# A transformer layer with experts on one core: feed-forward output as three split products, compact denominators, key epsilon by summed values, and a new order of each batch's work

## The reference

```python
xp = einsum(x * norm, proj); diag = sum(x**2) * 0.5 * norm**2      # per head
stab = max(xp, -1) if is_query else max(xp, (-1, -2))
feature = ratio * (exp(xp - diag - stab) + EPS_K)                  # EPS_K = 1e-4; qp, kp
k_sum = sum(kp, tokens); denom = qp . k_sum; ctx = kp^T v
out = (qp . ctx) / denom
x = layer_norm(video + out @ Wo.T + bo, g2, be2)
ff = relu(x @ W1.T + b1) @ W2.T + b2
x = layer_norm(x + ff, g3, be3)
```

## Time and profile before

| | |
|---|---|
| median of 3 runs | 826.82 us (825.84 to 826.87) |
| the profiled execution | 828.11 us, span 826.1 us |
| mean granted clock of TensorE | 0.917 |
| busy, share of the span | PE 85%, DVE 74%, ACT 57%, POOL 45% |
| starts of batches 0, 1, 2, 4 and 7 on TensorE | 14.13, 77.52, 135.76, 253.70, 430.41 us |
| last feed-forward's first hidden chunk | 493.47 us |
| selection | 538.3 to 599 us |
| experts, then the last normalisation | from 599 us |

### The profile page before, as it was taken

One profiled execution on the slowest core, in us unless ns is written; L12 is line 12 of the kernel. 1 busy time (PEld: TensorE's weight loads), 2 busy tenths in 40 slices (PEclk: granted clock), 3 DMA queues, 4 the chain that ended last, 5 costly groups with the idle time before them and its releaser, 6 DMA issues. The chain is left out here.

```text
span 826.1 us, 15455 instructions
## 1 busy us (share of the span) xinstructions
PE 703.9 (85%) x5669; PEld 571.6 (69%) x5669; DVE 612.1 (74%) x1279; ACT 474.6 (57%) x753; POOL 370.1 (45%) x364
## 2 busy tenths in 40 slices
PE   4777999999999999999999979632599999999930
PEld 3655867868768768768768758522488899998830
DVE  4637659878978978978888797777776777678671
ACT  2553674875875875866867834354055444455461
POOL 4065341662564544536527512400244565454673
PEclk9867999999999999999999999755599999999975
DMA  7000001012012011011011011250136644556694
GB/s 244 2 2 26 2 2 52 1 52 70 10 52 78 0 69 59 25 51 52 25 51 28 27 52 52 66 174 0 46 116 154 157 113 112 133 149 160 155 236 100
DMA packets 50700, 60.97 MB, mean 74 GB/s; under 512 B 9312, under 2 KB 44896, under 8 KB 50656
## 3 DMA queue, kind: packets, MB, share of 16 engines
q1 hardware_dynamic: 42400, 46.45, 17.3%
q0 software_dynamic: 7296, 13.77, 8.8%
q10 hardware_dynamic: 960, 0.17, 0.1%
HBM read 39.28 MB, written 21.10 MB: 73 GB/s over the span
## 5 line engine op out<-in xcount | busy, mean ns | idle before, releaser
L1907 PE MATMUL pF<-w,h 128*128 128x256 f32 x448 | 106.0, 382 | 0.0
L1004 POOL DMA_INDIRECT kp<-row_scratch,idx_g x32 | 41.5, 1298 | 117.5 <-issue 60.3
L1907 PEld LDWEIGHTS pF<-w,h 128*128 128x128 f32 x448 | 81.8, 190 | 13.1 <-issue 3.4
L793 ACT ACTIVATE h<-pX,b1cur 128x512 f32<-128x512 f32 x64 | 44.1, 689 | 62.9 <-DVE b1cur L1697 45.6
L2205 PE MATMUL pX<-w_lo,h_hi 128*128 128x256 f32 x256 | 73.2, 286 | 0.8 <-issue 0.8
L2205 PE MATMUL pX<-w_hi,h_lo 128*128 128x256 f32 x256 | 72.4, 283 | 0.0
L2205 PE MATMUL pX<-w_hi,h_hi 128*128 128x256 f32 x256 | 72.4, 283 | 0.0
L881 POOL TENSOR_SCALAR ve<-mv 128x4 f32<-128x4 f32 x36 | 8.5, 235 | 140.6 <-DVE mv L1082 139.5
L1653 DVE TENSOR_TENSOR h_lo<-h,h_hi 128x512 fp32r<-128x512 f32 x64 | 42.9, 690 | 29.3 <-ACT h_hi L785 29.3
L1012 POOL DMA_INDIRECT acc_scratch<-qp,idx_s x28 | 53.1, 1897 | 22.6 <-DVE qp L1679 18.3
L1844 PE MATMUL pX<-x2T_hi,w_lo 128*128 128x512 f32 x128 | 51.6, 403 | 1.6 <-DVE x2T_lo L1723 1.6
(11 more groups left out here) (375 smaller groups left out, 2098.2 us busy)
## 6 DMA issues: line engine op xcount, KB each, us to landing
kp<-fc1T SPq DMA_DIRECT2D x8, 1024.0 KB
w<-fc2T SPq DMA_DIRECT2D x8, 1024.0 KB
xin<-video SPq DMA_DIRECT2D x8, 512.0 KB, 3.8
x<-video SPq DMA_DIRECT2D x7, 512.0 KB, 4.5
out<-x SPq DMA_DIRECT2D x7, 512.0 KB, 3.0
acc_scratch<-xf SPq DMA_DIRECT2D x7, 512.0 KB, 2.9
row_scratch<-y SPq DMA_DIRECT2D x7, 512.0 KB, 3.0
kp<-acc_scratch SPq DMA_DIRECT2D x4, 512.0 KB, 6.5
```

The source lines that it names most:

```text
L793: nc.scalar.activation(h[:, n, :], pM[n % M_SLOTS], ACT.Gelu_apprx_tanh, bias=b1cur[:, n:n + 1]).then_inc(he_ready, 1)
L1004: pool.indirect_dma_start(xg[:, g, :], None, row_d, bass.IndirectOffsetOnAxis(ap=idx_g[:, g:g + 1], axis=0)).then_inc(gathered, 16)
L1907: ins = nc.tensor.matmul(pF[m][:, half * D:(half + 1) * D], h[:, k, tok(2 * m + half)], w2[:, k, :], start=(k == 0), stop=(k == FC - 1))
```

## The change

1. The feed-forward output becomes three split products in the experts' form: `h_hi*w2_lo` and `h_hi*w2_hi` (`ff_top`), later `h_lo*w2_hi` (`ff_low`), 96 fp32r products of 128x256 a batch. ScalarE makes `h_hi` (eight copies of 128x512), VectorE `h_lo` over `h` (eight subtractions, `rest_of_hidden`, in the order `low(n)`); `w2` is split once in batch 0. The end stage does the same in half width.
2. Denominators of all heads go into one 128x128 tile (nine groups of four products), one reciprocal follows, and a selector product spreads it over `pX`; ScalarE copies the outputs out of PSUM, VectorE multiplies.
3. The key epsilon is no longer added to `kp`: GpSimd sums the four value slices (`vsum`, 128x512 and 128x256), and the contexts and the denominators get a group of products with an epsilon column.
4. Each engine's order is new, below for VectorE, GpSimd and TensorE. SP loads inputs two batches ahead. Buffers are shared anew (x2 is r's, the heads' halves are the query squares', `h_lo` lies over `h`); three constants of the selection are built after the last rows instead of ahead of batch 0; the experts' second weights and half of the accumulators have buffers of their own.

```diff
 # VectorE, body
-                if u is not None and not (isinstance(u, int) and u == 0):
-                    scores(u - 1)
...
+                k_max(i, 0)
+                k_max(i, 1)
...
+                norms(i, 0, dgk)
+                norms(i, 1, dgk)
+                k_max(i, 2)
+                k_max(i, 3)
...
                     stats(3, su, z)
+                low(0)
+                low(1)
+                q_max(i, 0)
+                q_max(i, 1)
+                low(2)
+                k_top(i, sa)
+                low(3)
...
+                k_shift(i)
+                k_sub(i, 0)
+                rest_of_squares(i)
+                q_max(i, 2)
+                q_max(i, 3)
+                k_sub(i, 1)
+                rest_of_tops(i)
+                k_sub(i, 2)
+                k_sub(i, 3)
+                for n in range(4, FC):
+                    low(n)
...
                     residual(u, su)
...
+                sums_of_context(i, sa)
+                if more and not (isinstance(i, int) and i == 0):
+                    ln1_stats(i + 1)
+                context_of_heads(i, sa)
                 if f is not None:
                     add_ff(0)
...
+                reciprocals(i)
+                heads_out(i, 0)
+                heads_out(i, 1)
+                rest_of_heads(i, 0)
...
+                rest_of_heads(i, 1)
...
+                    add_ff(1)
+                    dve.wait_ge(z_ready, 2 * (f + 1))
+                attention_sum(i, 0)
+                attention_sum(i, 1)
 # GpSimd, body, behind x2 * g2
+                if f is not None:
+                    pool.wait_ge(x2b_ready, 2 * f + 1)
+                    nc.gpsimd.tensor_tensor(x2[:], x2[:], b2_b[:].unsqueeze(1).to_broadcast([P, TT, D]), ALU.add).then_inc(x2b_ready, 1)
                 if u is not None:
                     root(3, u)
                     shift(3, u, nz)
...
+                    if not (isinstance(i, int) and i == 0):
+                        with_bias(i)
+                    pool.wait_ge(v_ready, 2 * i + 2)
+                    halves = v.rearrange("p (k a) d -> p k (a d)", k=2)
+                    nc.gpsimd.tensor_tensor(vsum.rearrange("p n x -> p (n x)"), halves[:, 0], halves[:, 1], ALU.add).then_inc(vsum_ready, 1)
+                    pool.wait_ge(vsum_ready, 2 * i + 1)
+                    nc.gpsimd.tensor_tensor(vsum[:, 0], vsum[:, 0], vsum[:, 1], ALU.add).then_inc(vsum_ready, 1)
                     for t in range(1, TT):
...
                         nc.gpsimd.tensor_tensor(ksum, kp[:, 0, :] if t == 1 else ksum, kp[:, t, :], ALU.add).then_inc(ksum_ready, 1)
 # ScalarE, body
+                exp_k(i, 0)
+                q_tops(i)
+                for t in range(1, TT):
+                    exp_k(i, t)
+                    if ut and t < 3:
+                        z_norm(u, 2 * t - 2)
+                        z_norm(u, 2 * t - 1)
 # TensorE
+                    for k in range(k0, k1):
...
+                        for n, w_ in enumerate((w2_lo, w2_hi)):
+                            nc.tensor.matmul(dst, h_hi[:, k, rows], w_[:, k, :], start=(half == 0 and k == 0 and n == 0), stop=False)
...
+                    for p in range(PAIRS + 1):
+                        for b in range(TT):
+                            w_, x_ = (denbd[:, p, :], qp[:, p, tok(b)]) if p < PAIRS else (densum[:], eps)
+                            ins = nc.tensor.matmul(s[32 * b:32 * b + 32, 0:P], w_, x_, start=(p == 0), stop=(p == PAIRS), tile_position=(0, 32 * b))
```

More of the change, by code:

```diff
@@ L185, in build @@
         gT = sb("gT", [P, P])
-        h = sb("h", [P, FC, N])
+        rec = gT
+        with ExitStack() as raw:
+            h = raw.enter_context(nc.sbuf_tensor("h", [P, FC, N], F32))
+        h_lo = sb("h_lo", [P, FC, N], F32R)
+        h_hi = sb("h_hi", [P, FC, N], F32R)
         w1_raw = h[:].rearrange("p a b -> p (a b)")[:, 0:C * FF].rearrange("p (c n) -> p c n", c=C)
@@ L419, in load_x, with body, outputs @@
                 sp.dma_start(xin[:], vid_d[i]).then_inc(xin_in, 16)
[L421 to L427, removed]
+            def body(i, more):
+                outputs(i - 2, i + 2 if more else None)
+            def outputs(u, n):
                 wait(sp, x1_out, 16 * u)
@@ L452, in _ @@
                 sp.dma_start(dst[:], src.rearrange("(c p) -> p c", p=P), allow_slow_non_contiguous=True).then_inc(wff_in, 16)
-            batches(sp, body)
-            outputs(L2)
-            sp.dma_start(b1e[:], b1s).then_inc(b1e_in, 16)
+            for n in range(1, 4):
+                load_x(n)
+            body(2, True)
+            with sp.Fori(3, B - 2) as i:
+                body(i, True)
+            body(B - 2, False)
+            body(B - 1, False)
+            outputs(L2, None)
+            score_rows(L2)
             def load_expert(e):
@@ L655, in body @@
                 if ut:
                     xf_norm(u)
-                if att:
-                    act.wait_ge(obias_ready, i + 1)
-                    wait(act, al_ready, i * C)
-                    for g in range(G):
-                        take_a(i, J_DEN + g, den[:, g, :], ACT.Identity, den_ready, bias=obias[:, 1, g:g + 1])
+                if not is_last(i):
+                    x_norm(i + 1)
+                act.wait_ge(obias_ready, i + 1)
+                for g in range(G):
+                    take_a(i, J_OUT + g, outs[:, g, :], ACT.Identity, outs_ready, bias=obias[:, g:g + 1])
@@ L896, in z_affine, with with_bias @@
                 nc.gpsimd.tensor_tensor(z[:], z[:], be3_b[:].unsqueeze(1).to_broadcast([P, TT, D]), ALU.add).then_inc(za_ready, 1)
+            def with_bias(i):
+                wait(pool, r_ready, i * 2)
+                pool.wait_ge(xn_ready, (i + 1) * TT)
+                nc.gpsimd.tensor_tensor(xnb[:], xn[:], bo_b[:].unsqueeze(1).to_broadcast([P, TT, D]), ALU.add).then_inc(xnb_ready, 1)
             def root_rows(u):
@@ L1394, in end_low, with end_rest @@
                 nc.vector.tensor_tensor(x2T_lo[:, :, cols(m)], pX_end(m), x2T_hi[:, :, cols(m)].bitcast(F32), ALU.subtract).then_inc(x2l_ready, 1)
+            def end_rest(m, n0, n1):
+                for n in range(n0, n1):
+                    dve.wait_ge(h_hi_ready, (L1 + m) * FC + n + 1)
+                    nc.vector.tensor_tensor(h_lo[:, n, cols(m)], h[:, n, cols(m)], h_hi[:, n, cols(m)].bitcast(F32), ALU.subtract).then_inc(h_lo_ready, 1)
             def end_affine(m):
@@ L2153, in _ @@
             end_out(1)
[L2154 to L2156 removed]
+            turned_xf(L2)
             end_turn(0)
```

615 lines of the change are left out of this document (307 added, 308 removed).

## The result

The changed kernel takes 868.21 us (median of 4 runs, 865.78 to 869.03) where the kernel before, beside it, takes 826.85: a ratio of 1.0496 [1.0471, 1.0521], 41 us slower. The forecast was 862, so the sign and nearly the size were right; two terms of the sum had the wrong sign (batch 0 by 6.5 us, batch 1 by 1.2), and inside a batch three sizes were off in ways that cancelled.

What follows compares the result with a forecast made beforehand. TensorE's list was taken to bound each batch, with VectorE's waits on GpSimd added. Batch 0 -4, batch 1 +0.9, batches 2 to 6 +31.5, batch 7 +4.3, end +2.9: +35.6 on 828.1, less 1.3, gives 862; range 850 to 870.

Steps and rivals of the forecast that it cites:

- rival 1: Batches: the exclusion doesn't bite, TensorE's list is the period, 57.8 a batch, 816 us in all; chance 0.19.
- First come, first served: VectorE's two-SBUF-input operations and GpSimd's additions exclude one another; whichever asks first runs, the other waits until it ends.
- rival 2: VectorE keeps the port through operations in a row and GpSimd waits: +2.6 to 4.1 a batch, 841 to 848; chance 0.15.
- Rival 4: Split products run at f32 price, 0.222 instead of 0.122 us each: +9.6 a batch, 930 in all; chance 0.01.
- batch 0, -4 forecast: Batch 0: shorter reciprocals on its chain, against `w2`'s split and a longer line of products: -4, between -1 and -7.
- the five places: TensorE's waits before `spread_kmax`, `turn_tops`, contexts, `ff_low` and denominators: 1.9, 1.3, 1.3, 0.85 and 2.8 us a batch.
- the feed-forward products: TensorE, each batch: 96 fp32r products in 11.70 us replace four f32 groups of 14.2: -2.5.
- Rival 3: TensorE's clock falls after longer gaps, beside the forecast's waits: +1.3 a batch, 871; sign: clock below 0.95 in batches 2 to 6; chance 0.05.
- place A: Key maximum: VectorE held up by GpSimd, so TensorE waits 1.9 us before `spread_kmax` and 1.3 before `turn_tops`.
- place B: Key features: `k_sub` and `low` stand for `ksum`; TensorE waits 1.3 at contexts, 0.85 at `ff_low`, 2.8 at denominators.
- The last stages: Last feed-forward half to the experts: half-width subtractions on VectorE against shorter TensorE outputs: +2.9, between 0 and +5.

Runs made afterwards that it cites:

- experiment 1: The changed kernel with the three key sum additions of a batch moved from GpSimd to VectorE: 840.21 us.
- experiment 2: The changed kernel with the key sum additions on GpSimd cut to 64 columns, the other 960 left out: 831.15 us.
- experiment 5: The changed kernel with GpSimd's `with_bias` moved to the head of its list from batch 1 on: 855.38 us.
- 6 to 8: Three reorderings of the changed kernel, each built on the one before: exclusion heeded (821.58 us), tail reordered too (820.34), batch 0 back in the first one's order (817.53).
- experiment 8: The changed kernel reordered to heed the exclusion, with a new tail order except in batch 0: 817.53 us, ratio 0.9880 to the kernel before.
- experiment 3: The changed kernel with, in batch 0 alone, GpSimd's last step of `w1`'s split waiting until VectorE has written the heads' rests: 860.92 us.
- experiment 4: The changed kernel with 20 extra TensorE products, never read, ahead of the denominators from batch 2 on: 863.40 us.

## Why the prediction came out right, and where it failed

**The mechanism was right.** It said that TensorE's list would lose a microsecond a batch and that VectorE, held up by GpSimd at two places, would release it late by more. Experiments 1, 2 and 5 show both places and their cause. 6 to 8 keep all the work of the change and come to 58.8 and then 57.9 a batch, where rival 1 had 57.8; but they change the order of the tail too, and what each part is worth was not taken apart. TensorE's work itself fell by less than said: 57.42 in a batch of experiment 8 against 58.06, 0.64 and not 1.15.

**The order.** First come, first served was read off one `nf` between two VectorE operations; it decided between the forecast and rival 2. After, two `k_sub` that stand in a row take 4.55 with a `ksum` in between, and the `ksum`s take 3.08 and 6.02 for 2.4 each alone: each side waits for the one that runs, and neither goes first through a row of its own. That holds for these long additions. A small GpSimd operation did stand through a row: behind the batches, `ve` (128x4, 0.23 alone) at 552.35 took 0.87 and ended at 553.22, after three `h_lo` of VectorE that stood in a row from 552.07 to 553.13. Rival 2 (841 to 848) fell, and so did rival 1 (816); its time is near that of experiment 8, where the exclusion is taken out of the way, though not by its terms: batch 0 gave 8.3 there (5 in rival 1) and the end cost 4.1 (1.9). Rival 4 fell: the split products start 0.12 us apart where they stand in a row, as in the earlier trace rows.

**Failed: batch 0, -4 forecast, +2.46 measured.** The prediction let the shorter reciprocals (0.96 for 6.7) bring the heads forward and counted one new subtraction, `w2`'s, as something that "can meet a `ksum`". It did not look at what the reciprocals had been hiding. VectorE, and GpSimd, in batch 0 of the kernel before:

```profile
71.60 1.66 DVE L1148 TENSOR_TENSOR aT_lo<-qe,aT_hi 128x512 fp32r<-128x512 f32 x2
```

```profile
49.76 2.37 POOL L942 TENSOR_TENSOR sq<-kp 128x1024 f32<-128x1024 f32 x1
52.27 4.87 POOL L942 TENSOR_TENSOR sq<-sq,kp 128x1024 f32<-128x1024 f32 x2
...
66.92 4.51 POOL L959 TENSOR_TENSOR w_lo<-h,w_hi 128x2048 fp32r<-128x2048 f32 x1
```

There `w1`'s split ended at 71.43, the moment at which the slow reciprocals let the rests begin. After, the split ends at 73.92, later by 2.5, since the `ksum`s ahead of it are held up themselves (3.06 and 7.54 for 2.37 and 4.87, among `k_sub`s and `w2`'s subtraction: 3.4 longer, of which 0.9 was made good by an earlier start); and the rests, ready at 69.69, stand until then. Experiment 3 takes that away and batch 0 falls to 59.41, 3.98 below the one before: the -4 of the forecast.

**Sizes that cancelled.** That 862 came within some 6 us of 868 is in part luck. In batches 2 to 6 the period was to be 65.2 and was 64.92 on average, but not from these terms. The waits were to be 8.5; batch 4 has 1.11, 0.74, 0.99, 0.21 and 2.67 at the five places and 0.23 in one other, 5.95. `spread_kmax` (1.11 for 1.9), `turn_tops` (0.74 for 1.3), the contexts (0.99 for 1.3) and `ff_low` (0.21 for 0.85) were over-sized by 2.3 together. Each was the difference of two long sums of durations, and small errors of a sum are large in a difference (`sdiag` was done 25.2 us after the batch's start and not 25.7). The work was to be 56.9 and was 57.88 in batch 6 (63.79 less 5.91 of waits), against 58.06 before: TensorE's list lost 0.2 and not 1.15. The term that was too small is the feed-forward products. Taken from the start of each piece to what follows it, waits left out, they are 13.2 for 14.6 before, -1.4 and not -2.5: the 11.70 of the earlier trace rows is the price of 96 in one row, and here they stand in nine pieces, three of which end in a wait. And the clock, which the forecast left out, gives 1.3 to 1.6 in four of the five batches.

**Rival 3 came partly true, beside the forecast and not in its place.** Its sign was to be a clock column under 0.95 in batches 2 to 6. Batches 2 to 5 show 0.97, but the 3.1 us behind the denominators' wait 0.50, and experiment 4 prices it. Its size (+1.3 a batch) was right, and its total, 871, lies nearer to the measured 868 than the forecast's 862; the sign that I set was too coarse, as it averages 3 us over 65.

**The other stages.** Batch 1 has no place A and got 0.29 shorter where +0.9 was forecast; with the additions cut short (experiment 2) it takes 56.33 for 57.95, so place B costs it 1.6. The last stages lose 4.58 for 2.9. Of these 1.06 is a wait for `h_lo` at 543.33 and 1.89 a longer one for `h` at 549.28 (2.85 for 0.96); the other 1.6 were not traced to one place, and no experiment touched them (109.3 to 110.5 in all eight).

## What to carry to other kernels

When operations are moved, write beside each stretch which of GpSimd's operations and which of VectorE's two-SBUF-input operations will be in flight together: their busy times don't show that each will stand for the other's whole length. Put GpSimd's long ones beside reductions, statistics and operations that read PSUM (in experiment 8 `xnb` ran in 2.42 beside four-slice statistics in 1.41, and `z` times its gain in 2.39 beside key maxima in 2.34: nobody stood), or move a short chain of additions to VectorE although it is the busier engine: three additions a batch were worth 28 us here. And before a long operation is shortened, look at what ended while it ran: that is what is late next.

## What the runs showed of the hardware that was not expected

- Very small operations stand until the other ends as well: `sdiag`, 16x16 with one SBUF tensor, took 0.92 under the first `vsum` (to 293.26), 0.40 in experiment 5, where the second `vsum` ended 0.37 after it began, and 0.22 in the earlier trace rows; `csum_own`, 128x4, took 1.97 in batch 0 behind `xnb`, 0.16 in batch 4. The Trainium skill, SBUF — State Buffer, section Who interferes with whom, says that a `tensor_scalar` can, when its operands meet the conditions, enter a mode in which it contends with GpSimd; the 0.92 agrees, though no run here shows which mode `sdiag` was in.
- The clock behind the gap of 2.60 to 2.68 us before the denominators fell to 0.50 in four of batches 2 to 6 after, in three of five in experiment 3 and two of five in experiment 5, and stayed at 1.00 in the others; behind 1.34 to 1.44 (experiment 1) it never fell. What sets the difference at the same gap is open.
- 20 useless products a batch made the kernel 5 us faster (experiment 4).
